# GpSimd's waits for the finished tables moved into the general path's loop, and tiles 0 and 1 picked between the list parts

## What is computed

```python
def gcn_conv(x, edge_index, W, b, n_nodes):
    ...
    norm = dinv[src] * dinv[dst]
    h = x @ W.T
    msg = h[src] * norm[:, None]
    out = jax.ops.segment_sum(msg, dst, num_segments=n_nodes)
    return out + b
...
h = gcn_conv(layernorm(x), edge_index, W1, b1)
out = gcn_conv(relu(h), edge_index, W2, b2)
x = x + out
x = x + soft_moe_ffn(layernorm(x))
```

## Time and profile before

| | |
|---|---|
| runs | 2760.42, 2765.11, 2767.28 us (median 2765.11) |
| profiled execution, its span | 2760.88 us, 2759.1 us |
| TensorE matmul, VectorE, GpSimd busy | 77%, 66%, 67% of the span |
| ScalarE busy | 19% |
| mean granted clock of TensorE | 0.923 |
| stage of the lists and tables | until 216.28 us |
| gathers of layer 1, first to last issue | 216.28 to 1365.68 us |
| gathers of layer 2, first to last issue | 1394.15 to 2541.6 us |

### The profile page before, as it was taken

One profiled execution on the slowest core, in us unless ns is written; L12 is line 12 of the kernel. 1 busy time (PEld: TensorE's weight loads), 2 busy tenths in 40 slices (PEclk: granted clock), 3 DMA queues, 4 the chain that ended last, 5 costly groups with the idle time before them and its releaser, 6 DMA issues.

```text
span 2759.1 us, 27636 instructions
## 1 busy us (share of the span) xinstructions
PE 2117.5 (77%) x7712; PEld 1252.4 (45%) x7713; DVE 1807.6 (66%) x2350; ACT 535.5 (19%) x985; POOL 1840.4 (67%) x1853
## 2 busy tenths in 40 slices
PE   6716778777778778787758888888877888788888
PEld 6703444444444444444424544444544544445334
DVE  7755666666766666666646666666666676667226
ACT  7950111111111111111101222112222221222210
POOL 3156777777777777777667777777777777776000
PEclk9997998999998999999868999999999999999899
DMA  9498999999999999999879999999999999998838
GB/s 330 155 412 284 322 318 327 318 320 323 323 328 328 328 324 324 324 320 318 281 262 323 371 344 339 339 345 343 342 344 341 343 340 341 334 339 315 265 106 327
DMA packets 237825, 876.71 MB, mean 318 GB/s; under 512 B 63260, under 2 KB 64044, under 8 KB 237756
## 3 DMA queue, kind: packets, MB, share of 16 engines
q0 software_dynamic: 143808, 671.74, 69.1%
q1 hardware_dynamic: 66132, 162.17, 16.1%
q10 hardware_dynamic: 27836, 42.21, 4.2%
HBM read 826.10 MB, written 82.00 MB: 329 GB/s over the span
## 4 chain that ended last, share of the span: by engine, by line
DMA 30%; POOL 26%; PE 16%; issue 16%; DVE 8%; ACT 4%; POOLq 0%; DVEq 0%; ACTq 0%; SPq 0%
DMA rows<-table_layer,gidx 27%; POOL rows L664 25%; PE work L1365 5%; DVE acc L1122 5%; PE left L1391 3%; PE left L1440 2%; DMA table_layer<-xstage 2%; ACT logits L729 1%; ACT xsT L718 1%; DVE agg L1122 1%; PE acc L1489 1%; PE fixed L1489 1%; DVE agg L1167 1%; PE left L1489 1%; PE work L1377 1%
## 5 line engine op out<-in xcount | busy, mean ns | idle before, releaser
L664 POOL DMA_INDIRECT rows<-table_layer,gidx x1764 | 1761.6, 999 | 537.9 <-issue 460.4
L1122 DVE TENSOR_TENSOR acc<-acc,rows 128x768 f32<-128x768 f32 x1176 | 1134.3, 965 | 705.9 <-DMA rows<-table_layer,gidx 651.6
L1391 PE MATMUL left<-rows,hot 128*128 128x384 f32 x1960 | 861.9, 569 | 447.0 <-DMA rows<-table_layer,gidx 439.9
L1365 PE MATMUL work<-WT,aggT 128*128 128x384 f32 x2352 | 799.7, 498 | 39.7 <-DVE row_idx L1059 38.2
L1391 PEld LDWEIGHTS left<-rows,hot 128*128 128x128 f32 x1960 | 374.1, 212 | 790.9 <-DMA rows<-table_layer,gidx 619.9
L1365 PEld LDWEIGHTS work<-WT,aggT 128*128 128x128 f32 x2352 | 455.2, 195 | 384.0 <-DVE row_idx L1059 71.5
L788 ACT ACTIVATE acc<-rows 128x768 f32<-128x768 f32 x98 | 79.8, 814 | 674.7 <-DVE agg L1167 593.7
L818 ACT ACTIVATE aggT<-fixed 128x768 f32<-128x768 f32 x98 | 79.5, 811 | 503.3 <-PE fixed L1341 503.3
L805 ACT ACTIVATE xsT<-fixed 128x768 f32<-128x768 f32 x49 | 39.7, 811 | 458.0 <-PE fixed L1352 458.0
L798 ACT ACTIVATE ynext<-hid,dinv 128x768 f32<-128x768 f32 x49 | 45.8, 934 | 342.8 <-DVE hid L1137 342.8
L1167 DVE TENSOR_TENSOR agg<-left,agg 128x768 f32<-128x768 f32 x98 | 93.9, 958 | 8.8
(11 more groups left out here) (307 smaller groups left out, 1251.8 us busy)
## 6 DMA issues: line engine op xcount, KB each, us to landing
self_row<-table_layer SPq DMA_DIRECT2D x98, 384.0 KB, 6.6
rows<-table_layer,gidx POOLq DMA_INDIRECT x1764, 5.7
xstage<-in_x SPq DMA_DIRECT2D x67, 384.0 KB, 8.7
xs<-in_x SPq DMA_DIRECT2D x58, 384.0 KB, 7.5
xnew<-xs SPq DMA_DIRECT2D x49, 384.0 KB, 5.2
table_layer<-ynext SPq DMA_DIRECT2D x48, 384.0 KB, 5.1
table_layer<-xstage ACTq DMA_DIRECT2D x40, 384.0 KB, 11.6
xstage<-xnew SPq DMA_DIRECT2D x21, 384.0 KB, 5.5
```

What stands on the lines that cost most here:

```text
L664: pool.indirect_dma_start(rows[:, slot, :], None, table[l][0:ROWS, :], bass.IndirectOffsetOnAxis(ap=gidx[:, k % 2, slot:slot + 1], axis=0) ...
L1122: dve.tensor_tensor(acc[:, :, 0:H] if n < OWN - 1 else halves(agg[:, :]), acc[:, :, 0:H], halves(row), ALU.add).then_inc(S["added"], 1)
L1365: m = pe.matmul(work[:, h, 0:H], aggT[:, kc, :], WT[l][:, kc, h * H:(h + 1) * H], start=kc == 0, stop=kc == KC - 1)
L1391: m = pe.matmul(left[:, h, 0:H], hot[:, b, c, :], rows[:, slot, h * H:(h + 1) * H], start=c == 0, stop=c == LEFT - 1)
```

## The change

Four edits, without any change to what is computed:

1. GpSimd no longer waits for the finished table ahead of the general path. The waits stand inside its loop, behind the wait for `over_idx` and directly ahead of the general path's gather.
2. ScalarE moves the indices of tile 0 (`move_idx`) before it waits for the table of layer 1, not behind.
3. The picks of tiles 0 and 1 move from behind the list parts to between them: tile 0's behind part 0, tile 1's behind part 1, each with `mark_ends` of the next tile. TensorE's `find_left(0)` and `find_left(1)` move likewise.
4. VectorE's first `chunk_added`, which lets SP load the general path's 128 edges for layer 1, is given before the list parts.

```diff
         def over_dve(dve, l, nth, nth16, tile, tile16):
-            if l == 0:
-                dve.sem_inc(O["chunk_added"], 1)
-
@@ over_pool
                 pool.wait_ge(O["idx_ready"], nth)
                 pool.sem_inc(O["wait_taken"], 1)
+                if l == 0:
+                    pool.wait_ge(s["zeros_out"], 32)
+                for b in range(X_LANES if l == 0 else 2):
+                    pool.wait_ge(*((y_out[b], y_count(b)) if l == 0 else (L[0]["stored"][b], done_count(b, 2))))
                 pool.indirect_dma_start(over_rows, None, table[l][0:ROWS, :],
@@ gpsimd
-            for b in range(X_LANES):
-                pool.wait_ge(y_out[b], y_count(b))
-            pool.wait_ge(s["zeros_out"], 32)
             pool.wait_ge(s["starts_ready"], 1)
...
-                if l == 1:
-                    for b in range(2):
-                        pool.wait_ge(L[0]["stored"][b], done_count(b, 2))
@@ scalar
                     act.wait_ge(s["starts_ready"], 1)
+                    act.wait_ge(s["own_idx_ready"], 1)
+                    move_idx(0, 0)
                     for b in range(X_LANES):
                         act.wait_ge(y_out[b], y_count(b))
-                    act.wait_ge(s["own_idx_ready"], 1)
-                    move_idx(0, 0)
@@ vector
+            dve.sem_inc(O["chunk_added"], 1)
             dve.wait_ge(s["iotas"], 7)
             for part, ((t0, t1), landed) in enumerate(zip(WINDOW_PARTS, windows_in)):
...
+                if part < 2:
+                    if part == 0:
+                        dve.wait_ge(s["fixed_ready"], 2)
+                        for m in range(PARKED):
+                            dve.wait_ge(y_out[m], 16)
+                        mark_ends(0)
+                    for n in range(6):
+                        pick_left(part, n)
+                    mark_ends(part + 1)
             dve.sem_inc(s["own_idx_ready"], 1)
...
-                if l == 0:
-                    dve.wait_ge(s["fixed_ready"], 2)
-                    for m in range(PARKED):
-                        dve.wait_ge(y_out[m], 16)
-                    mark_ends(0)
-                    for n in range(6):
-                        pick_left(0, n)
-                    mark_ends(1)
                 mark_hot(0, 0)
                 over_dve(dve, l, *counts)
-                if l == 0:
-                    for n in range(5):
-                        pick_left(1, n)
                 dve.sem_inc(S["over_done"], 1)
-                if l == 0:
-                    pick_left(1, 5)
-                    mark_ends(2)
@@ tensor
+            pe.wait_ge(s["w_moved"], 2 * KC)
+            pe.wait_ge(s["fixed_ready"], 2)
             for part, (t0, t1) in enumerate(WINDOW_PARTS):
                 pe.wait_ge(s["sums_in"], 4 + part)
                 pe.matmul(cand_banks[part][:, 0:(t1 - t0) * (COLS - 1)], steps_down[:, :],
                           windows[:, t0:t1, OWN - 1:OWN + EXTRA], start=True, stop=True).then_inc(s["sums_out"], 1)
+                if part < 2:
+                    find_left(part)
```

More of the change, by code:

```diff
@@ L994, in _, with mark_ends, pick_left @@
             dve.sem_inc(s["slots_ready"], 1)
+            def mark_ends(t):
+                if not (isinstance(t, int) and t == 0):
+                    dve.wait_ge(L[0]["left_found"], t)
+                dve.tensor_scalar(before_end[:, 0:LEFT * P], slot_iota[:, 0:LEFT * P], left_end[:, ds(t, 1)], None, ALU.is_lt
+                                  ).then_inc(L[0]["ends_marked"], 1)
+            pick_halves = pick[:, :, :].rearrange("p (h c) n -> p h c n", h=2)
+            def pick_left(t, n):
+                c = L[0]["pick_step"]
+                if n == 0:
+                    dve.wait_ge(L[0]["left_found"], t + 1)
+                    dve.tensor_tensor(groups(pick_col[:, 0, :]), groups(slot_of[:, :]), found[:, :, :, 1],
+                                      ALU.subtract).then_inc(c, 1)
+                elif n == 1:
+                    dve.wait_ge(c, 5 * t + 1)
+                    dve.tensor_tensor(pick[:, :, :], pick_iota.unsqueeze(1).to_broadcast([P, PICKS, EXTRA]),
+                                      pick_col[:, 0, :].unsqueeze(2).to_broadcast([P, PICKS, EXTRA]),
+                                      ALU.is_equal).then_inc(c, 1)
+                elif n == 2:
+                    dve.wait_ge(c, 5 * t + 2)
+                    dve.tensor_tensor(pick_halves, pick_halves, found[:, :, :, 2:COLS], ALU.mult).then_inc(c, 1)
+                elif n == 3:
+                    dve.wait_ge(c, 5 * t + 3)
+                    dve.tensor_reduce(pick_col[:, 1, :], pick[:, :, :], AX.X, ALU.add).then_inc(c, 1)
+                elif n == 4:
+                    dve.tensor_scalar(groups(pick_col[:, 2, :]), found[:, :, :, 0], 0.0, FAR, ALU.is_equal, ALU.mult
+                                      ).then_inc(c, 1)
+                elif n == 5:
+                    dve.tensor_copy(left_node[:, ds(t, 1), :].rearrange("p t (h c) -> p (t h) c", h=2), found[:, :, :, 0])
+                    dve.wait_ge(c, 5 * t + 5)
+                    dve.tensor_tensor(row_idx[:, ds(t, 1), 0:LEFT], pick_col[:, 1, 0:LEFT].unsqueeze(1),
+                                      pick_col[:, 2, 0:LEFT].unsqueeze(1), ALU.add).then_inc(L[0]["left_ready"], 1)
+            dve.sem_inc(O["chunk_added"], 1)
             dve.wait_ge(s["iotas"], 7)
@@ L1300, in _, with find_left @@
             m.then_inc(s["slot_sums"], 1)
+            def find_left(t):
+                pe.wait_ge(L[0]["ends_marked"], t + 1)
+                if not (isinstance(t, int) and t == 0):
+                    pe.wait_ge(L[0]["left_ready"], t)
+                for c in range(LEFT):
+                    m = pe.matmul(found[:, c // 3, c % 3, :], before_end[:, c * P:(c + 1) * P], cands[:, ds(t, 1), :],
+                                  start=True, stop=True)
+                m.then_inc(L[0]["left_found"], 1)
+            pe.wait_ge(s["w_moved"], 2 * KC)
+            pe.wait_ge(s["fixed_ready"], 2)
             for part, (t0, t1) in enumerate(WINDOW_PARTS):
@@ L1308, in _ @@
                 S = L[l]
-                def find_left(t):
-                    pe.wait_ge(S["ends_marked"], t + 1)
-                    if not (isinstance(t, int) and t == 0):
-                        pe.wait_ge(S["left_ready"], t)
-                    for c in range(LEFT):
-                        m = pe.matmul(found[:, c // 3, c % 3, :], before_end[:, c * P:(c + 1) * P], cands[:, ds(t, 1), :],
-                                      start=True, stop=True)
-                    m.then_inc(S["left_found"], 1)
-                if l == 0:
-                    pe.wait_ge(s["w_moved"], 2 * KC)
-                    pe.wait_ge(s["fixed_ready"], 2)
-                    find_left(0)
-                else:
+                if l == 1:
                     pe.wait_ge(L[0]["scaled_ready"], T)
                 over_pe(pe, l, *counts)
-                if l == 0:
-                    find_left(1)
                 pe.wait_ge(S["over_done"], 1)
```

31 lines of the change are left out of this document (removed).

## The result

The changed kernel takes 2759.01 us (median of 20 runs, 2756.14 to 2761.98); the kernel before took 2764.22 beside it (20 runs, 2760.42 to 2768.85). The ratio is 0.9981, with a 95% interval of 0.9975 to 0.9987: 5.2 us less. That is under the 0.3% that the prediction held to be the least that can be told; with 20 runs of each kernel the interval does exclude no change.

The account below looks back on a forecast made before the run. GpSimd's back-to-back gathers were taken to bound both layers, so only earlier starts count: 3.1 us in layer 1 plus 1.35 in layer 2 make 4.45; 2763.4 less 4.4 gives 2759.0 us, range 2752 to 2766.

Parts of the forecast that it names:

- What bounds the kernel: Both layers: GpSimd issues gathers back to back, 1.304 us each; only each layer's first gather start and the tail count.
- Edit 1, layer 1: 0.8 from the last semaphore to the gather: Ahead of layer 1: general path's gather starts 0.8 us behind the table's landing, at 211.9 instead of 215.0, gaining 3.1.
- Edit 1, layer 2: 1.35: Ahead of layer 2: trip counts read early, so the general path's gather starts at 1391.5 instead of 1392.85, gaining 1.35 us.
- The bound from below: Wait-to-gather time before each layer: if the whole 0.8 us were hidden, each layer would gain 0.8 more.
- The index at 209.2 at the latest: VectorE's general-path index before layer 1 is ready by 209.2, 1.9 us before the table lands.
- The picks are hidden: Picks of tiles 0 and 1, moved between list parts, fit VectorE's idle time there and cost nothing.
- The 1.0 us that the prediction allowed for slower window gathers: Before layer 1: three marks beside GpSimd's window gathers could delay the last windows and the index by 1.0 us.
- Tile 0's start 4.0 earlier: Start of layer 1: TensorE's first left chunk starts at 218.7 instead of 222.66, 4.0 us earlier, adding no gain.
- The sum, 4.45: Whole kernel: gains of 3.1 us before layer 1 and 1.35 before layer 2 add to 4.45.
- The index is still last: Rival before layer 1: late edges or windows keep GpSimd waiting for VectorE; 2762.1 us if layer 1's gain is lost; chance 0.08.
- The clock helps: Rival at the layers' turn and layer 2's end: dense products run at 2.4 GHz, 4.1 us more gained, 2754.9; chance 0.08.
- hurts: Rival at the same two dense products: the lower clock adds up to 11.9 us, giving 2770.9, 7.5 slower; chance 0.06.

Follow-up runs that it names:

- s1_pause_layer: Changed kernel with one more GpSimd wait per tile in the layers' gathers, a pause of 4.5 us a tile: 3205.57 us, 1.1598 of the kernel before.
- v3_shifted_picks: Changed kernel with each pick one list part later and the zero rows' wait behind the table lanes' waits: 2758.03 us, 0.9981 of the kernel before.
- e3_late_edges: Changed kernel with the mark releasing SP's load of the 128 edges back behind all the lists: 3042.73 us, 1.0001 of the kernel before, same chip.
- b_after: Changed kernel, unaltered, on a chip with late TensorE notices: 3065.33 us, 1.0008 of the kernel before on that chip.
- e8: Changed kernel with 26 more TensorE matmuls ahead of the tail's mixing loop: 3049.41 us, 1.0019 of the kernel before on the same chip.
- v1_later_pick: Changed kernel with tile 1's pick moved one list part later, behind part 2: 3059.87 us, 0.9992 of the kernel before on the same chip.
- p1_pause: Changed kernel with GpSimd waiting for tile 1's find before its ninth window gather from the end: 3058.12 us, 0.9975 of the kernel before, same chip.

## Why the prediction was right, point by point

- **What bounds the kernel.** Right on the first chip and on S. The layers' lengths didn't move by more than 0.1 us, and `s1_pause_layer` shows that a layer has no slack to give.
- **Edit 1, layer 1: 0.8 from the last semaphore to the gather.** Right: 0.78.
- **Edit 1, layer 2: 1.35.** Mis-sized. The table landed at 1387.72 and the gather started at 1387.98, 0.26 behind it instead of 0.8; in the kernel before it was 2.18 (1390.67 to 1392.85). The gain is 1.92. The bound from below named it ("were the whole of it hidden"), and I took the other end, on a misreading: the prediction says that the trace has no gather whose wait came last and that started in less than 0.8, but the first window gather is one, 0.27 behind VectorE's notice (123.62 to 123.89; rows below). The wait for that notice is the first that the code lists for it. In layer 2 too the wait that ends last is the one that the loop lists first, and that one sits on the gather itself; in layer 1 the first listed is the zero rows', and lane 0's stands ahead. `v3_shifted_picks` exchanges the two and gets 0.26 in layer 1 as well. The difference is the 0.53 us of "issue" behind the wait in the chain above. The table's landing itself came 0.3 later behind the last gather (25.28 instead of 24.98), behind a dense product that took 0.4 longer, which leaves 1.63. The rows of before that the misreading passed over (chain of waits, then the timeline):

```profile
123.60 0.02 DVEq L942
...
123.89 1.07 POOL L633 DMA_INDIRECT rows<-src_windows,ynext  x1 [28.03 <-DVEq L942]
```

- **The index at 209.2 at the latest.** Right: 208.93. SP issues the edges at 197.6 instead of 210.3; that part is worth 1.15 us (`e3_late_edges`).
- **The picks are hidden.** Right on this chip: part 1 starts 0.4 later, parts 2 and 3 at the same time. The 1.0 us that the prediction allowed for slower window gathers did not come: those beside the three marks took 1.00 to 1.05, and the last of all starts at 188.76 (188.79 before). The term leaned on idle time of VectorE and on GpSimd's contention with it; the thing that could break it, a wait for TensorE amid GpSimd's gathers, was not among its risks. It costs 4 to 6 us ahead of layer 1 on chips P, Q and R (the general path's gather at 220.5 to 221.8 instead of 215.4 to 216.8).
- **Tile 0's start 4.0 earlier.** Only 2.8: TensorE's first left chunk starts at 219.88 (222.66 before). ScalarE's load of `agg` (L281, 212.05) and the general path's gather now run side by side, and the gather lands in 3.56 us instead of 2.08; in `v3_shifted_picks`, where the load follows the gather by 0.9 us instead of 0.4, it lands in 2.09. The gathers don't feel it.
- **The sum, 4.45.** 4.9 up to the last gather, 5.2 in the medians; 2759.0 predicted, 2759.01 measured. How close it came is partly luck: the base that I took, 2763.4, was 0.8 under the median that more runs gave, and the gain was 0.8 more than counted.
- **Rivals.** *The index is still last* did not happen here, and did on three other chips (`b_after`, `e3`, `e8`), by another cause than the two it named. *The clock helps* and *hurts*: the dense product at the turn took 10.79 (10.39 before) and that at the end 10.51 (9.67), 1.2 us more together, far from the 4.4 at which it decides.

## What to carry to other kernels

When one engine's stream of instructions bounds a stage, count a change by when that stream starts, and look at the last wait before it: put the semaphore that comes last on the instruction itself, so that its preparation is done by then (0.26 instead of 0.78 us here). Idle time into which work is moved is free only if what the work itself waits for comes in time, on every chip: here the moved work waits for an engine whose notices can come 11 us late, and a wait that comes when the notice is due anyway costs least (`v1_later_pick`: 0.04 us for tile 1's find instead of 12.9). A gain of 0.2% that hangs on such a place should be timed on more than one chip.

## What the runs showed of the hardware

- The same program takes 2764 us on two occasions and 3042 to 3064 on three other chips. There GpSimd's idle time inside the layers is 812.9 us instead of 537.9 (changed kernel, R), 2.8 us more a tile. In these pauses the first of TensorE's notices comes 2.2 us (layer 1, median of 46 pauses, 2.0 to 2.7 for nine in ten; 2.7 in layer 2) behind the end of GpSimd's last gather, and the others in a burst. That the pauses make up the 10% is argued from these sizes; no run took them away inside the layers.
- Tile 1's find is told 11 us late while GpSimd issues gathers back to back, and on time when it stands still (`p1_pause`, one find in one trace); some get through earlier (find 0, 3 to 8 us later than on the first chip). Whether it is the acknowledgement or the semaphore that is held, and why only on some chips, stays open. The traces of those chips also lack most landings of the layers' gathers (8,502 of 28,224 are recorded, all of them on the others), which is why so many rows say "remote".
